# Second attention's slot in another order, and the last FFN's first rows turned and multiplied inside the attention's drain

## The reference

```python
x = x + tanh(g_xattn[0]) * L0_xattn(layernorm(x), ctx, ...)
x = x + tanh(g_ffn[0])   * L0_ffn(layernorm(x), ...)
x = x + tanh(g_xattn[1]) * L1_xattn(layernorm(x), ctx, Wq, Wk, Wv, Wo, bo)
x = x + tanh(g_ffn[1])   * L1_ffn(layernorm(x), ...)

def L1_xattn(x, context, Wq, Wk, Wv, Wo, bo):      # 8 heads of 64
    q, k, v = split_heads(x @ Wq), split_heads(context @ Wk), split_heads(context @ Wv)
    attn = softmax(einsum('bhid,bhjd->bhij', q, k) * 64 ** -0.5)
    return merge_heads(einsum('bhij,bhjd->bhid', attn, v)) @ Wo + bo

def L1_ffn(x, ...):                                 # 256 -> 1024 -> 256
    h = butterfly(x @ W_exp + b_exp, up_weights)
    h = gelu(h + up_bias)
    return butterfly(h, down_weights) @ W_con + b_con + down_bias
```

## Time and profile before

| | |
|---|---|
| median of 3 runs | 1190.38 us (1187.0 to 1194.2) |
| the profiled execution | 1190.78 us, of which the span of the profile is 1189.0 us |
| PE busy | 1017.9 us (86%) |
| DVE busy | 793.4 us (67%) |
| ACT busy | 626.4 us (53%) |
| mean granted clock of PE | 0.912 |
| second attention's slots | about 696 to 976 us |
| butterfly FFN | about 978 to 1189 us |

### The profile page before, as it was taken

The page is one execution under the profiler, slowest core; times in us unless marked ns, Lnnn a source line. Parts: engine busy times, 40 slices in busy tenths (PEclk is TensorE's granted clock), DMA queues, the critical chain, the costliest instruction groups (busy, mean ns, idle before and its releaser), DMA issues. The chain is left out here.

```text
span 1189.0 us, 20552 instructions
## 1 busy us (share of the span) xinstructions
PE 1017.9 (86%) x6833; PEld 882.9 (74%) x6833; DVE 793.4 (67%) x1588; ACT 626.4 (53%) x1088; POOL 236.0 (20%) x423
## 2 busy tenths in 40 slices
PE   6499999998579997656899959999999968999998
PEld 5377777776468876445789948888898856888888
DVE  5357887864358988889588525666666557765662
ACT  3256666664378699789386434555555432222220
POOL 4212233321168000000023021111112012211110
PEclk9689999998789999767799967999999878999999
DMA  6735555552222167599133665454545410000101
GB/s 196 216 95 134 133 133 133 134 165 67 80 109 107 71 216 253 193 338 334 47 114 133 224 145 145 107 111 98 111 101 114 92 36 1 18 19 18 35 18 36
DMA packets 102807, 143.60 MB, mean 121 GB/s; under 512 B 42950, under 2 KB 76742, under 8 KB 100438
## 3 DMA queue, kind: packets, MB, share of 16 engines
q1 hardware_dynamic: 102438, 141.67, 41.2%
q0 software_dynamic: 304, 1.10, 0.3%
HBM read 76.30 MB, written 47.13 MB: 104 GB/s over the span
## 5 line engine op out<-in xcount | busy, mean ns | idle before, releaser
L41 PE MATMUL bank<-f_xt_hi,f_w_hi 128*128 128x512 f32 x320 | 131.5, 411 | 16.0 <-DMA f_xt_lo<-x_spill 8.8
L43 PE MATMUL bank<-f_xt_hi,f_w_lo 128*128 128x512 f32 x320 | 128.6, 402 | 0.0
L42 PE MATMUL bank<-f_xt_lo,f_w_hi 128*128 128x512 f32 x320 | 128.6, 402 | 0.0
L2482 ACT ACTIVATE f_h<-bank,f_b 128x512 f32<-128x512 f32 x64 | 43.4, 690 | 132.9 <-PE bank L43 85.3
L595 ACT ACTIVATE a_prob<-bank 77x512 f32<-77x512 f32 x128 | 72.7, 591 | 32.6 <-PE bank L759 32.2
L661 DVE TENSOR_REDUCE a_maxima<-bank 128x4 f32<-128x308 f32 x128 | 60.5, 473 | 43.9 <-PE bank L734 43.6
L41 PEld LDWEIGHTS bank<-f_xt_hi,f_w_hi 128*128 128x128 f32 x320 | 62.4, 195 | 32.4 <-DMA f_xt_lo<-x_spill 10.9
L41 PE MATMUL bank<-f_w_hi,f_h_hi 128*128 128x256 f32 x256 | 72.8, 284 | 7.2 <-DVE xres L2448 7.2
L756 PE MATMUL bank<-a_stack,a_kb 96*77 96x256 f32 x256 | 72.5, 305 | 4.7 <-ACT a_mt L588 4.7
L43 PEld LDWEIGHTS bank<-f_xt_hi,f_w_lo 128*128 128x128 f32 x320 | 62.2, 195 | 14.1
L43 PE MATMUL bank<-f_w_hi,f_h_lo 128*128 128x256 f32 x256 | 72.2, 282 | 0.0
(11 more groups left out here) (292 smaller groups left out, 3115.5 us busy)
## 6 DMA issues: line engine op xcount, KB each, us to landing
...
```

Source lines behind the costliest of these rows:

```text
L41: nc.tensor.matmul(out, w_hi, m_hi, start=start, stop=False)
L42: nc.tensor.matmul(out, w_hi, m_lo, start=False, stop=False)
L43: return nc.tensor.matmul(out, w_lo, m_hi, start=False, stop=stop)
L2482: act.activation(h[:, n % 2, :], hbank[n % 4][:, :], ACT.Gelu, bias=b1[:, n:n + 1]).then_inc(h_ready, 1)
```

## The change

It does three things. The steps of the attention's slot are put in another order, and their banks and waits are adapted: `xt` is made for batch b+2 at the end of the slot instead of for batch b+1 at its start, `q0` and `q1` move between the score steps, the maxima move from bank X0 to T0, `mx0` waits for the split of `q0` alone, and `s0` waits for both splits. In the drain, the layernorms of the FFN's first two groups are made (the first one slot earlier than before), the first group is transposed and split (`next_x`), and four of its eight `h` products are made (`next_h0` to `next_h3`, 24 products of 512 columns) between the attention's last steps, into the FFN's own banks. To have room, `xt_hi`, `xt_lo` and `xn` of the FFN are allocated before the attention, and the attention's `q_both` and `xn` are views of them. The FFN then begins with the transposes of group 1 and with `h` number 4.

```diff
-        PE_SLOT = "xt s0 s1 s2 q0 q1 at0 p0 p1 mx0 at1 mx1 p2 s3 mx2 pr0 mx3 p3 mt pr1".split()
-        ACT_SLOT = "xt s0 s1 q0 q1 at0 s2 at1 xn s3 mt".split()
-        DVE_SLOT = "xt ln q0 q1 at0 mx0 mx1 at1 mx2 mx3 norm pr1".split()
+        PE_SLOT = "s0 s1 q0 at0 s2 q1 mx0 p0 mx1 p1 at1 s3 mx2 p2 mx3 p3 mt pr0 xt pr1".split()
+        ACT_SLOT = "s0 s1 q0 at0 q1 s2 at1 s3 xn mt xt".split()
+        DVE_SLOT = "ln q0 at0 mx0 q1 mx1 mx2 at1 mx3 norm xt pr1".split()
-        PRE = {"ln", "xn"}
-        FRONT = {"xt", "mt", "qm"} | {f"q{n}" for n in range(NP)} | {f"mx{n}" for n in range(NG)}
+        PRE = {"ln", "xn", "xt"}
+        FRONT = {"mt", "qm"} | {f"q{n}" for n in range(NP)} | {f"mx{n}" for n in range(NG)}
...
-        xn = sb("xn", [P, TT, D])
+        xn = nxt.xn[:, 1, 0:TT, :]
-        q_both = [sb(f"q_both{a}", [P, 2, C, T], F32R, "right") for a in range(HPC)]
+        q_both = nxt.query_tiles
...
         def _(act):
+                elif what == "next_x":
+                    act.wait_ge(hi_in[0], B // 2 * 32 * HPC)
+                    act.wait_ge(hi_in[1], B // 2 * 32 * HPC)
+                    act.wait_ge(scores, B * HP)
+                    for c in range(DC):
+                        act.wait_ge(nxt.xt_ready, c + 1)
+                        act.activation(nxt.xt_hi[:, 0, c, :], turn_banks[c][:, :], ACT.Copy).then_inc(nxt.xt_rounded, 1)
...
             slots(act, ACT_SLOT, step,
-                  {(B - 1, "xt"): "turn0", (B - 1, "q0"): "turn1", (B - 1, "q1"): "turn2", (B - 1, "mt"): "turn3",
-                   (B, "s3"): "next_w2"})
+                  {(B - 1, "q0"): "turn0", (B - 1, "q1"): "turn1", (B - 1, "s2"): "turn2", (B - 1, "at1"): "turn3",
+                   (B - 1, "xn"): "next_x", (B, "s3"): "next_w2"})
...
             slots(dve, DVE_SLOT, step,
-                  {(B - 1, "ln"): "next_ln", (B - 1, "xt"): "turn0", (B - 1, "q0"): "turn1", (B - 1, "q1"): "turn2",
-                   (B - 1, "mx3"): "turn3", (B, "ln"): "next_xn", (B, "norm"): "next_w2"})
+                  {(B - 2, "ln"): "next_ln0", (B - 2, "pr1"): "next_xn0", (B - 1, "ln"): "next_ln1",
+                   (B - 1, "q0"): "turn0", (B - 1, "q1"): "turn1", (B - 1, "mx1"): "next_xn1",
+                   (B - 1, "mx2"): "turn2", (B - 1, "at1"): "turn3", (B - 1, "mx3"): "next_x", (B, "norm"): "next_w2"})
...
         def _(pe):
+                elif what == "next_x":
+                    pe.wait_ge(nxt.ln_xn, 1)
+                    for c in range(DC):
+                        pe.wait_ge(nxt.w1_split, c + 3)
+                        for t in range(GTT):
+                            last = pe.transpose(turn_banks[c][:, t * P:(t + 1) * P], nxt.xn[:, 0, t, c * P:(c + 1) * P],
+                                                ident[:])
+                        last.then_inc(nxt.xt_ready, 1)
+                elif what[:6] == "next_h":
+                    m = int(what[6])
+                    if m == 0:
+                        pe.wait_ge(nxt.xt_split, DC)
+                        pe.wait_ge(probs, B * HP)
+                    if m == 2:
+                        pe.wait_ge(att_ready, B)
+                    for c in range(DC):
+                        last = three_passes(nc, nxt.h_banks[m][:, :], nxt.w1_hi[:, c, m * P:(m + 1) * P],
+                                            nxt.w1_lo[:, c, m * P:(m + 1) * P], nxt.xt_hi[:, 0, c, :],
+                                            nxt.xt_lo[:, 0, c, :], c == 0, c == DC - 1)
+                    last.then_inc(nxt.h_sum, 1)
...
-                        pe.wait_ge(q_split, (b + 1) * NP)
+                        pe.wait_ge(q_split, b * NP + 1)
+                    elif g == 1:
+                        pe.wait_ge(q_rounded, (b + 1) * NP)
...
             slots(pe, PE_SLOT, step,
-                  {(B - 1, "xt"): "turn0", (B - 1, "q0"): "turn1", (B - 1, "q1"): "turn2", (B - 1, "mt"): "turn3"})
+                  {(B - 1, "q0"): "turn0", (B - 1, "q1"): "turn1", (B - 1, "p1"): "turn2", (B - 1, "s3"): "turn3",
+                   (B - 1, "mx3"): "next_x", (B, "s0"): "next_h0", (B, "s2"): "next_h1", (B, "s3"): "next_h2",
+                   (B, "xt"): "next_h3"})
...
 def butterfly_ffn(nc, env, out):
-                    if front and m == 6:
+                    first = isinstance(g, int) and g < 0
+                    if front and m == (0 if first else 6) and not (first and g == -2):
                         step("x", 0, g + 2, par)
...
+                    if isinstance(g, int) and g == 0 and n < nxt.EARLY:
+                        return
```

More of the change, by code:

```diff
@@ L955, in slot @@
                         step(what, b, par)
-                    if isinstance(b, int) and b >= B - 1 and (b, what) in prepare:
+                    if isinstance(b, int) and (b, what) in prepare:
                         step(prepare[b, what], 0, 0)
@@ L1054, in step @@
                     last.then_inc(biased, 1)
-            slots(pool, POOL_SLOT, step, {(B - 1, "ln"): "next_ln"})
+            slots(pool, POOL_SLOT, step, {(B - 2, "ln"): "next_ln0", (B - 1, "ln"): "next_ln1"})
         @block.scalar
@@ L1296, in step @@
                         at = (HPC * n - h0) * S
-                        last = pe.matmul(X0[:, at:at + HPC * S], q_hi[:, n, t * P:(t + 1) * P],
+                        last = pe.matmul(T0[:, at:at + HPC * S], q_hi[:, n, t * P:(t + 1) * P],
                                          kz[:, par, n, :, :].rearrange("p a s -> p (a s)"), start=True, stop=True)
@@ L2416, in step @@
                 if what == "ln":
[L2417 to L2418 removed]
+                    if isinstance(g, int) and g < 2:
+                        if g == 0:
+                            dve.tensor_scalar(gb[:], ob[:, 0, :], tg[:, 0:1], None, ALU.mult).then_inc(gb_ready, 1)
                         return
@@ L2463, in _ @@
             rest(0)
-            with pool.Fori(1, G) as g:
+            rest(1)
+            with pool.Fori(2, G) as g:
                 pool.wait_ge(ln_stats, g + 1)
@@ L2494, in step @@
                         for t in range(GTT):
-                            last = pe.transpose((T0, T1)[c][:, t * P:(t + 1) * P], xn[:, t, c * P:(c + 1) * P],
+                            last = pe.transpose((T0, T1)[c][:, t * P:(t + 1) * P], xn[:, par, t, c * P:(c + 1) * P],
                                                 ident[:])
@@ L2562, in build @@
                 quantised_ffn(nc, env, env["ffn_weights"]["quantised"], a["gf0"], butterfly)
-            env["next"] = NextFfn(nc, next_stack, butterfly["w1_dram"], butterfly["w2_dram"], a["up_bias"],
+            env["next"] = NextFfn(nc, next_stack, [env["banks"][n] for n in (4, 5, 3, 2)], butterfly["w1_dram"], butterfly["w2_dram"], a["up_bias"],
                                   a["out_bias"], a["gf1"])
```

57 lines of the change are left out of this document (35 added, 22 removed).

## The result

| | kernel before | kernel after |
|---|---|---|
| median of the runs | 1192.29 us (1187.0 to 1194.9) | 1143.81 us (1142.95 to 1147.79) |
| profiled execution, span | 1190.8, 1189.0 | 1144.3, 1142.5 |
| granted clock, whole span | 0.91 | 0.93 |

The ratio is 0.9605, 95% interval 0.9563 to 0.9648. The profiled pair differs by 46.5 us where the sum said 35.8.

The account below looks back on a forecast made before the run. PE's own list was taken to bound the attention loop, with single waits and the clock behind it. Gains of 16.8 + 3 + 3 + 2 + 11 = 35.8 us from 1190.8 gave 1155 us, range 1146 to 1172.

Parts of the forecast that it names:

- the sum: Whole kernel: the gains of 16.8, 3, 3, 2 and 11 us added to 35.8 us, giving 1155 us.
- The steady slot: Attention loop: reordered steps remove PE's waits, 1.2 us a slot, fourteen slots, 16.8 us (10 to 19.5).
- The clock: Attention loop: falls to half clock cost 7 us, of which 3 us (between 0 and 7) come back.
- the rival of a fall in every slot: Attention loop: the clock falls once in each slot, 26 us more, 1184 us, about no change; chance 0.08.
- The filling: Slots -1, 0 and 1 of the attention: 3 us (0 to 6) over the 1.2 already counted.
- The walk: New slot stepped through from `s0`: PE's issue time sets it, 13.7 to 13.9 us, with small margins for the waits.
- a DMA margin: Before `s0` in each slot: the four DMAs land at 12.8, needed at 13.9, 1.1 us to spare.
- The drain: Slot 15 to DVE's last addition, 27.6 us before: 2 us gained (-1 to 3.5).
- In slot 16 no wait over 0.5: Drain, a sign of the forecast: no wait over 0.5 us in slot 16, each `h` group covering a round trip.
- The FFN's start: First transposes to group 0's last addition: 48.1 us falls to 36.5, three slow splits counted; 11 us taken (4 to 13).

## Why the prediction was right in direction and short in size

- **The steady slot: the step that failed.** "The excess is 0.34 + 0.43 + 0.37 = 1.14 us. The later maxima lose a little too, so 1.2 us a slot, a slot of 13.9", with 13.7 called the least. It is 13.5, the gain 1.5. Two numbers in that line were wrong, and both from taking a row for something that it isn't. A score step behind other products is 0.465 (847.39 to 848.32 for two), not the 0.53 that I read from one that stands behind a wait; that hid 0.13. And "0.82 where `mx0` is busy 0.45" took the length of the row for its issue time, which is 0.29: `at1` waited 0.53, not 0.37. Together 0.3, which times 14 is 4 of the 11 us that were missing, nearly all of what the steady slots lack.
- **The clock: the second miss.** "No row shows how it falls, so between 0 and 7 I take 3 us back." All 7 came back. The row to look at was the 0.37 idle before `at1`, in the middle of the thin steps. Filling that one gap in the kernel before took the falls away; a gap in the thin steps of the kernel after brought them, in five of twelve slots; gaps ahead of dense steps, of 0.47 to 1.4 us in two kernels, did not; nor did a longer thin stretch with next to no gap. So the rival of a fall in every slot argued from the bunching, which does not do it, and the removed waits were worth more than their own length. Two things stay open. Most of these readings rest on one profile of each kernel, and whether it is the gap itself or the sparse work in the whole stretch around it that counts isn't told apart.
- **The filling** came out 1.4 above "3 us", its bounds held. The DMA waits of 0.82 and 1.95 in slots 0 and 1 were in no step of mine; that the stage gained all the same goes with its clock. From the first transposes to `s0` of slot 2 it is 0.78 against 0.70 before, so by an estimate from these two PE was at half clock for 20 us instead of 31, worth up to 5 us, as much as the term. Why it fell less there was not tested.
- **The walk** was right in structure: no wait before `mx0`, `s1`, `s2`, `at1`, and a DMA margin that is real but small.
- **The drain** was right by its total (1.5 for 2) and wrong inside: the order gives 5.3, the moved work takes 3.9, and DVE's early normalising makes about 2 of that (26.2 with it, 24.0 without). "In slot 16 no wait over 0.5" held; the waits of 0.69 and 0.47 were in slot 15.
- **The FFN's start** was right: 36.7 us where the walk said 36.5, with two slow splits for its three.
- **Upstream** gave 1.7 us that belong to no part of the change and lie within what this stretch varies from run to run. That is luck, in the direction of the gain.

By the Trainium skill (TensorE: Matmul & The Clock Gate, Part 4: PE-mode transpose), transposes don't count as activity that brings the full clock. By that rule the eight added ones would have made the drain's term about 0. That did not come: with them the clock from ACT's last `xt` copy to the end of the drain was 0.96 (0.92 in the second profile of the kernel after), and 1.00 in the two versions with the normalising moved, which have the same transposes without the two waits among them. The waits alone don't decide it either. The kernels with `xt` at the start, with the bunched thin steps, with the longer thin stretch and with the gap in the thin steps have them too (0.7 to 1.5 us and 0.5), and their drains show 1.00 behind them. In three profiles of the seven with the waits the clock fell there, in neither of the two with the normalising moved.
